# Sixteen chained accumulating scatters in place of a one-hot combination matmul

## The chip, the cores and the metric

One core of one Trainium2 chip runs the whole program. The metric is the device time in microseconds. Beside plain executions there is one profiled execution, from which all rows come.

## What is computed

Two transformer layers on x of 8 images x 256 tokens x 192 channels (2048 tokens in all):

```python
x = x + neighbourhood_attention(ln(x))                 # 12 heads, 7x7 window
t = t + routed(ln(t)) + shared(ln(t))                  # layer 0 mixture of experts
x = x + window_attention(ln(x))                        # rows of 16 tokens
h = x + causal_attention(rms(x)); out = h + moe(rms(h))  # layer 1, 16 experts, top 2
```

The change concerns the routed part of layer 0. Of 32 experts each token chooses 6; an expert keeps at most 48 tokens (CAP), the rest is dropped:

```python
buf_idx = where(pos < CAP, se * CAP + pos, E * CAP)
token_buf = zeros(E * CAP).at[buf_idx].set(tok_of_pair, mode='drop')
xb = x[token_buf].reshape(E, CAP, H)
yb = (silu(g) * u) @ W_down * w_buf[..., None]
routed = zeros((T, H)).at[token_buf].add(yb.reshape(E * CAP, H))
```

## The kernel before, in words

All engines run programs of their own, ordered by semaphores alone; the order of work on each engine is written out by hand. The stages follow each other:

- Stage A, per image: neighbourhood attention, router of layer 0, shared expert. SyncE stores the normalised rows with their router weights (`rows0`), and per image writes zeros over an eighth of `sorted_x` (line 895). TensorE makes slot tables; at the end `ids_f` holds for each of 16 expert pairs (NPAIR) and 128 slots the token's number. A pair has two experts of 64 slots each.
- Stage B, the experts: GpSimd gathers the 16 sets of rows (line 996). The loop `b_body` runs over 8 steps of two pairs: gate and up (lines 1746, 1751), activation, gate product on VectorE (1335), transposes (1765), down (1776). SyncE loads the weights into a ring of five, each load as soon as its slot is read (877, 880). VectorE scales the result by the slot weights into `y_f` (1341), frees the accumulator (`b_yc`), and splits `y_f` into three bf16 parts in `y0_all` (1347 to 1350).
- Stage C, per image: combine, window attention, causal attention, router of layer 1, scatter to `sorted_x` (1031). The combine of an image is `c_comb`: 96 bf16 matmuls of 128 x 128 by 192 (line 1796) with one-hot matrices `comb_s`, which GpSimd compares from `ids_rel` (`c_onehot`, line 1010, 16 per tile and 32 per image); VectorE adds the sum to `x_all` in `c_combine` (1366) and takes the statistics. GpSimd also computes the reciprocal roots of the norms (970, 971), in the same queue as the one-hots.
- In stage C the images overlap by hand: the combine of images 0 and 1 stands ahead of and in the first window attention; in the turn of image i (0 to 5) the combine of image i + 2 stands as 24 matmuls (EARLY_COMB = 8 of 32 steps) ahead of `c_head` and as 72 behind the causal projections (line 1826). The turns of images 6 and 7 have none. VectorE calls `c_combine` of image i + 2 inside the causal attention (`between[1]`).
- Stage F: the 16 experts of layer 1 over 48 sorted tiles; weights of 864 KB a tile, results scattered to `token_y` (1058); then everything is read back, added and stored.

Of the kernel before, what the change touches and what calls it, by code (L numbers as in the profile page):

```python
# [23 lines left out]
P = 128  # L24
# [45 lines left out]
def _lay(table, items):  # L70
    at = 0
    for name, n in items:
# [5 lines left out]
NCF = _lay(CF, [("ident", P), ("iota_slot", CAP), ("iota_tok", P), ("cos", 2 * HD), ("sin", 2 * HD),  # L78
                ("tiles", 16), ("sorted", NSORT), ("half", 2), ("neg", 6), ("back", 1), ("place", NT + 2), ("experts", E1), ("spread", P), ("regions", E1), ("limit", 2), ("dump", 4)])
# [4 lines left out]
def constants():  # L84
# [9 lines left out]
    put(f, CF, "iota_tok", np.arange(P))  # L94
# [9 lines left out]
    put(f, CF, "back", -P)  # L104
# [67 lines left out]
A_FIRST, A_TAIL, C_FIRST = 7, 3, 14  # L172
LINKS = {"A": 32, "B": 5, "C": 62}
C_SHORT = 3
EARLY_COMB = 8


def build(nc, d, out):
    ctx = ExitStack()
    with ctx:  # L180
# [87 lines left out]
        y0_all = y0_words.bitcast(BF16).rearrange("p (j s c) -> p j s c", j=NPAIR, s=3)  # L268
# [14 lines left out]
        comb_s = hT_words.bitcast(BF16).rearrange("p (t j k) -> p t j k", t=2, j=NPAIR)  # L283
# [21 lines left out]
        ids_rel = sb("ids_rel", [P, NPAIR])  # L305
# [57 lines left out]
        token_y = nc.dram_tensor("token_y", [2 * TOK + 2 * P, C], F32)  # L363
        rows0_t = rows0[:, :].rearrange("(i t p) c -> i p t c", t=2, p=P)
# [33 lines left out]
        for n in ("cf_loaded", "cb_loaded", "x0_loaded", "x1_loaded", "x_loaded", "wqkv_loaded", "wproj_loaded", "router_loaded",  # L398
# [4 lines left out]
                  "b_idf", "b_weights", "b_link", "b_done",  # L403
                  "c_onehot", "c_comb", "c_link", "c_var", "c_u", "c_ss", "c_rstd", "c_xn", "c_xT", "c_xTc",
# [5 lines left out]
        for j in range(NPAIR // 2):  # L410
            s(f"b_rows{j}")
        for j in range(RING):
            s(f"ring_gu{j}")
            s(f"ring_dn{j}")
# [445 lines left out]
        def _(sp):  # L860
# [29 lines left out]
            sp.dma_start(sx[NBLOCK - 1], empty).then_inc(s("zeroed"), 16)  # L890
            with sp.Fori(0, B) as i:
# [75 lines left out]
        def _(pool):  # L967
# [31 lines left out]
            pool.wait_ge(s("a_done"), B + 1)  # L999
# [6 lines left out]
            def c_onehot(link, i, t):  # L1006

                nc.gpsimd.tensor_tensor(scratch[:, 9:10], cst("back"), cst("back"), ALU.add)
                for j in range(NPAIR):
                    ins = nc.gpsimd.tensor_scalar(comb_s[:, t, j, :], cst("iota_tok"), ids_rel[:, j:j + 1], None,  # L1010
                                                  ALU.is_equal)
                ins.then_inc(s("c_onehot"), 1)
                pool.wait_ge(s("c_onehot"), 2 * i + t + 1)
                link(nc.gpsimd.tensor_tensor(ids_rel[:, :], ids_rel[:, :], cst("back").to_broadcast([P, NPAIR]),
                                             ALU.add))
            link = Links(pool, s("c_pool"), 0, 8)
# [19 lines left out]
            def c_body(i, level):  # L1036
# [10 lines left out]
                if level == 2:  # L1047
                    c_onehot(link, i + 3, 1)
# [946 lines left out]
```

## Time and profile before

| what | us |
|---|---|
| median of 3 runs (range) | 1319.44 (1316.85 to 1319.55) |
| profiled execution, its own time | 1314.41 |
| its span, first to last instruction | 1312.6 |
| stage A to the first gather | 409.9 |
| stage B, first gather to the last `y_f` | 409.9 to 512.3 |
| stage C to the last scatter of rows | 512.3 to 1094.8 |
| stage F and the end | 1094.8 to 1312.6 |

The mean granted clock of TensorE over the span is 0.94. Read the stages apart: A and F are untouched but for added zero-writes in A; B and C are where every edit lies.

### The profile page before, as it was taken

The numbers are of one execution on the slowest core, as the hardware profiler recorded it, in microseconds if no ns is written. First come the engines' busy times: TensorE is split into PE (matmuls) and PEld (weight loads), VectorE is DVE, ScalarE is ACT, GpSimd is POOL, SyncE is SP. The second block draws the span as 40 slices with busy tenths as digits, with TensorE's granted clock in tenths as the row PEclk, the third lists the DMA queues.
The fourth block names the chain that finished last, engine by engine and source line by source line (L and its number), as shares of the span: only waits on it lengthen the run. The fifth ranks groups of instructions, "written<-read, shape, count | busy, mean of one in ns | idle before, by whom it ended". The sixth has DMA issues, their size and how long they took to land.

```text
span 1312.6 us, 27217 instructions
## 1 busy us (share of the span) xinstructions
PE 1043.5 (80%) x9541; PEld 805.9 (61%) x9573; DVE 747.4 (57%) x2308; ACT 481.1 (37%) x1205; POOL 347.6 (26%) x581
## 2 busy tenths in 40 slices
PE   4899999999987997767777787878767563999992
PEld 3676677677765555646556565656545353888882
DVE  6677668668643443437676767666666644233334
ACT  2454354355342221314454545454535341121120
POOL 0000000000003700683544444444530101233322
PEclk8999999999988999779999999999999775999997
DMA  9044044144229993000000000000000005888885
GB/s 343 13 137 136 3 134 136 33 103 136 59 76 248 372 423 126 0 17 1 15 2 16 0 16 0 16 0 16 0 17 1 17 0 191 270 304 279 281 306 165
DMA packets 69203, 144.73 MB, mean 110 GB/s; under 512 B 4960, under 2 KB 55424, under 8 KB 66848
## 3 DMA queue, kind: packets, MB, share of 16 engines
q1 hardware_dynamic: 64352, 132.76, 30.6%
q0 software_dynamic: 4800, 11.32, 2.6%
q8 instruction: 30, 0.49, 0.2%
q14 instruction: 21, 0.17, 0.0%
HBM read 97.22 MB, written 46.83 MB: 110 GB/s over the span
## 4 chain that ended last, share of the span: by engine, by line
issue 33%; PE 27%; POOL 17%; DVE 12%; ACT 5%; DMA 5%; POOLq 1%; DVEq 0%; ACTq 0%; SPq 0%
POOL R L1010 10%; PE bank L1659 4%; DMA R<-in_ffn_gu 3%; PE bank L577 2%; PE bank L1687 2%; POOL rstd L971 2%; POOL sorted_x L1031 2%; PE bank L595 2%; DVE neg_max L673 2%; PE bank L637 2%; POOL token_y L1058 1%; ACT R L702 1%; PE bank L1796 1%; PE bank L536 1%; PE bank L1746 1%
## 5 line engine op out<-in xcount | busy, mean ns | idle before, releaser
L702 ACT ACTIVATE R<-bank,neg_max 128x128 f32<-128x128 f32 (+2 forms) x576 | 187.6, 410 | 78.1 <-DVE neg_max L673 77.5
L1010 POOL TENSOR_SCALAR R<-cf,ids_rel 128x128 bf16<-128x128 f32 x288 | 187.1, 667 | 0.1
L970 POOL TENSOR_TENSOR rstd<-mean_var,cf 128x2 f32<-128x2 f32 x32 | 6.2, 195 | 612.7 <-DVE mean_var L840 612.4
L673 DVE TENSOR_REDUCE neg_max<-bank 128x2 f32<-128x352 f32 (+2 forms) x216 | 130.1, 611 | 53.5 <-PE bank L560 44.2
L577 PE MATMUL bank<-cf,R 128*128 128x128 f32 x864 | 134.3, 278 | 21.2 <-ACT R L702 12.4
L577 PEld LDWEIGHTS bank<-cf,R 128*128 128x128 f32 x864 | 93.7, 141 | 40.0 <-ACT R L702 13.3
L724 ACT ACTIVATE R<-bank 128x1024 bf16<-128x1024 bf16 x72 | 70.2, 1017 | 106.5 <-PE bank L536 106.5
L1659 PE MATMUL bank<-R 64*116 64x256 f32 (+1 forms) x512 | 97.4, 398 | 0.0
L1574 DVE TENSOR_TENSOR R<-R,bank 128x384 f32<-128x384 f32 x48 | 26.6, 555 | 108.1 <-ACT R L1154 105.4
L1882 PE MATMUL bank<-xsT,R 128*128 128x128 f32 x576 | 75.9, 285 | 13.1 <-DMA R<-in_ffn_w 11.4
L536 PE MATMUL bank<-cb,R 128*128 128x128 bf16 x1008 | 67.5, 230 | 21.8 <-DVE R L521 21.8
L560 PE MATMUL bank<-R 128*128 128x128 bf16 (+2 forms) x576 | 79.4, 243 | 5.3 <-issue 4.6
L1882 PEld LDWEIGHTS bank<-xsT,R 128*128 128x128 f32 x576 | 70.5, 197 | 19.1 <-DMA R<-in_ffn_w 10.9
L1659 PEld LDWEIGHTS bank<-R 64*116 64x116 f32 (+1 forms) x512 | 65.2, 180 | 26.1 <-issue 16.4
L536 PEld LDWEIGHTS bank<-cb,R 128*128 128x128 bf16 x1008 | 62.8, 104 | 28.7 <-DVE R L521 17.9
L1154 ACT ACTIVATE R<-bank 128x384 f32<-128x384 f32 x48 | 23.6, 491 | 142.6 <-PE bank L1889 142.6
L711 ACT ACTIVATE R<-bank 128x512 f32<-128x512 f32 (+2 forms) x152 | 64.4, 461 | 15.1 <-PE bank L577 15.1
L557 PE MATMUL bank<-cb 128*128 128x352 bf16 (+1 forms) x184 | 65.8, 357 | 3.6 <-ACT R L724 3.2
L1796 PE MATMUL bank<-R 128*128 128x192 bf16 x768 | 66.0, 247 | 2.6 <-DVE R L1350 2.6
L560 PEld LDWEIGHTS bank<-R 128*128 128x128 bf16 x576 | 53.0, 103 | 24.6 <-issue 3.6
L1796 PEld LDWEIGHTS bank<-R 128*128 128x128 bf16 x768 | 64.1, 98 | 4.9 <-DVE R L1350 3.0
L595 PE MATMUL bank<-R 128*32 128x128 f32 x1152 | 49.9, 280 | 17.3 <-ACT R L711 17.0
(251 smaller groups left out, 1954.9 us busy)
## 6 DMA issues: line engine op xcount, KB each, us to landing
R<-in_ffn_w SPq DMA_DIRECT2D x48, 864.0 KB, 6.3
sorted_x<-cmp SPq DMA_DIRECT2D x8, 4128.0 KB, 16.9
R<-in_ffn_gu SPq DMA_DIRECT2D x16, 1392.0 KB, 21.3
R<-in_ffn_dn SPq DMA_DIRECT2D x16, 768.0 KB, 18.6
xs_words<-sorted_x SPq DMA_DIRECT2D x48, 129.0 KB, 2.8
R<-token_y SPq DMA_DIRECT2D x8, 384.0 KB, 6.8
rows<-R SPq DMA_DIRECT2D x8, 224.0 KB, 2.2
out_x<-x_all SPq DMA_DIRECT2D x16, 96.0 KB, 2.4
```

The source lines that it names most:

```text
L536: ins = nc.tensor.transpose(bank[:, :].bitcast(BF16)[:, (h * 2 + t) * P:(h * 2 + t + 1) * P], qk_parts[:, row, :, :].rearrange("p s e -> p ...
L557: nc.tensor.matmul(bank[:, 0:len(heads) * kw], cstb("identb"), cstb(mname, moff, len(heads) * kw), start=True, stop=False)
L560: ins = nc.tensor.matmul(bank[:, g * kw:(g + 1) * kw], q_ap(h, t), k_ap(a, h, k0, kw), start=False, stop=(g == len(heads) - 1))
L577: ins = nc.tensor.transpose(PT[u % 2][:, at + g * P:at + (g + 1) * P], probs[:, u % 3, g * kw + c0:g * kw + c0 + P], ident)
L595: ins = nc.tensor.matmul(OB[t][j * HV:(j + 1) * HV, col:col + P], v_ap(a, h, vt), probsT[:, u % 4, at + g * P:at + (g + 1) * P], start=(k ...
L673: nc.vector.tensor_reduce(neg_max[:, u % 4, 0:g], score_bank(u)[:, 0:g * kw].rearrange("p (g k) -> p g k", g=g), AX, ALU.max, negate=True) ...
L702: ins = nc.scalar.activation(probs[:, u % 3, g * kw:(g + 1) * kw], score_bank(u)[:, g * kw:(g + 1) * kw], ACT.Exp, bias=neg_max[:, u % 4, ...
L724: nc.scalar.activation(qkT[:, h0:h0 + heads, :].rearrange("p h t -> p (h t)"), bank[:, :].bitcast(BF16)[:, 0:heads * 256], ACT.Copy, scale ...
L1010: ins = nc.gpsimd.tensor_scalar(comb_s[:, t, j, :], cst("iota_tok"), ids_rel[:, j:j + 1], None, ALU.is_equal)
L1659: ins = nc.tensor.matmul(GATE[g % 3][part][0:DP0, c * 256:(c + 1) * 256], wsgu[rows, 2 if k else part, at:at + DP0], xnT_all[rows, k, :], ...
L1796: ins = nc.tensor.matmul(M1[:, t * C:(t + 1) * C], comb_s[:, t, j, :], y0_all[:, j, k, :], start=(j == 0 and k == 0), stop=(j == NPAIR - 1 ...
L1882: nc.tensor.matmul(GU[r][part][:, c * P:(c + 1) * P], w[:, part * FF + c * P:part * FF + (c + 1) * P], xsT[:, r, 0, :], start=(c == 0), st ...
```

## The change

The 128 weighted rows of a pair, `y_f`, are no longer kept as three bf16 parts. GpSimd adds them to a table `routed` in memory with an accumulating indirect DMA. The table has two halves of 2048 rows, one for the first expert of each pair (slots 0 to 63) and one for the second, and 128 rows behind them for empty slots; so the rows of one scatter are all different. Sixteen scatters run strictly one behind the other (`b_sum`), since two of them can add to the same row. VectorE waits for both scatters of the step before it writes `y_f` again. The table is zeroed by SyncE beside `sorted_x`. Behind the last scatter SyncE loads both halves back per image into `sums` (16 loads of 192 KB), and `c_combine` adds two tiles from there in place of one accumulator. One-hots, the combination matmuls and the bf16 splits are gone. The diff, without the tables of constants, semaphores and tile declarations:

```diff
@@ SyncE
+            sp.dma_start(routed[2 * TOK:2 * TOK + P, :], empty[:, 0:C]).then_inc(s("sum_zeroed"), 16)
             with sp.Fori(0, B) as i:
                 sp.wait_ge(s("a_row"), i + 1)
...
+                sp.dma_start(routed_z[bass.ds(i, 1)].rearrange("a p n c -> (a p) n c"),
+                             empty[:, 0:C].unsqueeze(1).to_broadcast([P, 4, C])).then_inc(s("sum_zeroed"), 16)
...
+            sp.wait_ge(s("b_sum"), 16 * NPAIR)
+            for i in range(B):
+                for k in range(2):
+                    sp.dma_start(sums[:, i, k, :, :], routed_i[i][:, k, :, :]).then_inc(s(f"sum_loaded{min(i, 2)}"), 16)
@@ GpSimd
-            pool.wait_ge(s("a_done"), B + 1)
+            pool.wait_ge(s("sum_zeroed"), 16 * (B + 1))
+            for j in range(NPAIR):
+                pool.wait_ge(s("b_ready"), j // 2 + 1)
+                if j:
+                    pool.wait_ge(s("b_sum"), 16 * j)
+                pool.indirect_dma_start(out=routed[:, :], out_offset=bass.IndirectOffsetOnAxis(ids_s[:, j:j + 1], 0),
+                                        in_=y_f[:, j % 2, :], in_offset=None, compute_op=ALU.add)\
+                    .then_inc(s("b_sum"), 16)
...
-            for i in range(3):
-                if i:
-                    pool.wait_ge(s("c_comb"), 2 * i)
-                    c_root(link, "c_var", i, mv, EPS6)
-                for t in range(2):
-                    c_onehot(link, i, t)
+            for i in range(2):
+                c_root(link, "c_var", i + 1, mv, EPS6)
...
                 if level == 2:
                     c_root(link, "c_var", 2 * i + 4, mv, EPS6)
-                    pool.wait_ge(s("c_comb"), 2 * i + 6)
-                    c_onehot(link, i + 3, 0)
                 c_root(link, "c_ss", 2 * i + 2, ss, EPS6)
-                if level == 2:
-                    c_onehot(link, i + 3, 1)
@@ VectorE
-            nc.vector.tensor_copy(ids_rel[:, :], ids_f[:, :])
             nc.vector.tensor_copy(ids_i[:, :], ids_f[:, :]).then_inc(s("b_idf"), 1)
+            nc.vector.scalar_tensor_tensor(ids_d[:, :], ids_f[:, :], cst("acc"), ids_acc[:, :, 2], ALU.add, ALU.mult)\
+                .then_inc(s("b_link"), 1)
+            dve.wait_ge(s("b_link"), 3)
+            nc.vector.tensor_scalar(ids_s[:, :], ids_d[:, :], cst("limit")[:, 0:1], None, ALU.add)
...
                 dve.wait_ge(s("b_y"), jj + 1)
-                link(nc.vector.tensor_tensor(y_f[:, :, :], two(M1[:, 0:2 * C]),
-                                             wsl[:, bass.ds(2 * jj, 2)].unsqueeze(2).to_broadcast([P, 2, C]), ALU.mult))
...
+                if jj:
+                    dve.wait_ge(s("b_sum"), 32 * jj)
+                nc.vector.tensor_tensor(y_f[:, :, :], two(M1[:, 0:2 * C]),
+                                        wsl[:, 2 * jj:2 * jj + 2].unsqueeze(2).to_broadcast([P, 2, C]), ALU.mult)\
+                    .then_inc(s("b_ready"), 1)
                 nc.vector.memset(scratch[:, 14:15], 0.0).then_inc(s("b_yc"), 1)
-                link(nc.vector.tensor_copy(part(0), y_f[:, :, :]))
-                link(nc.vector.tensor_tensor(y_f[:, :, :], y_f[:, :, :], part(0), ALU.subtract))
-                link(nc.vector.tensor_copy(part(1), y_f[:, :, :]))
-                link(nc.vector.tensor_tensor(part(2), y_f[:, :, :], part(1), ALU.subtract))
...
             def c_combine(link, i):
-                dve.wait_ge(s("c_comb"), 2 * i + 2)
-                link(nc.vector.tensor_tensor(image_x(i), image_x(i), two(M1[:, 0:2 * C]), ALU.add))
+                if isinstance(i, int):
+                    dve.wait_ge(s(f"sum_loaded{i}"), 32)
+                for k in range(2):
+                    link(nc.vector.tensor_tensor(image_x(i), image_x(i), sums[:, bass.ds(i, 1), k, :, :]
+                                                 .rearrange("p a t c -> p (a t) c"), ALU.add))
...
+            dve.wait_ge(s("sum_loaded2"), 32 * (B - 2))
@@ TensorE
-            pe.wait_ge(s("b_done"), LINKS["B"] * (NPAIR // 2))
...
-            c_comb(0, 0, 2 * NPAIR)
             c_head(1)
...
-            attention_pe(pe, WINDOW, 0, {2: lambda: c_comb(1, 0, 2 * NPAIR), (WINDOW.n, "transposed"): lambda: c_head(2)})
+            attention_pe(pe, WINDOW, 0, {(WINDOW.n, "transposed"): lambda: c_head(2)})
...
-                if level == 2:
-                    c_comb(i + 2, 0, EARLY_COMB)
...
-                if level == 2:
-                    c_comb(i + 2, EARLY_COMB, 2 * NPAIR)
```

## Rows read from the trace of the kernel before

**Rows 1.** The longest pieces of the chain that ended last: start us, us, what

```profile
514.30 8.11 PE bank L1796 x96
545.98 7.92 PE bank L1796 x96
570.36 9.27 POOL R L1010 x16
```

**Rows 2.** Windows A:B: length, busy us of each engine (instructions), clock, DMA share, GB/s

```profile
436.10:512.30 76.20, 70.66 (x564) 37.79 (x560) 32.79 (x70) 15.41 (x27) 14.95 (x25) 1.00 0.91 360
909.90:974.70 64.80, 47.62 (x473) 36.40 (x477) 44.01 (x141) 30.60 (x82) 29.65 (x49) 0.97 0.02 8
974.70:1039.30 64.60, 39.77 (x381) 28.86 (x385) 40.09 (x128) 30.07 (x81) 6.84 (x11) 0.89 0.03 9
977.00:986.00 9.00, 3.78 (x11) 2.27 (x10) 6.42 (x25) 0.00 (x0) 2.06 (x3) 0.69 0.14 46
1115.70:1281.00 165.30, 153.47 (x1399) 142.93 (x1398) 52.90 (x218) 33.72 (x88) 49.77 (x85) 1.00 0.84 286
```

**Rows 3.** Timeline, VectorE: start us, us, instruction; first and last y_f, first combine

```profile
436.08 0.56 DVE L1341 TENSOR_TENSOR y_f<-bank,wsl 128x384 f32<-128x384 f32 x1 [2.43 <-PE bank L1776]
...
511.71 0.56 DVE L1341 TENSOR_TENSOR y_f<-bank,wsl 128x384 f32<-128x384 f32 x1 [2.07 <-PE bank L1776]
...
522.53 0.56 DVE L1366 TENSOR_TENSOR x_all<-x_all,bank 128x384 f32<-128x384 f32 x1 [8.29 <-PE bank L1796]
```

**Rows 4.** Timeline of the end, GpSimd's scatter and VectorE's wait for it

```profile
1286.53 0.99 POOL L1058 DMA_INDIRECT token_y<-y_f,place_i  x1 [0.16 <-POOL scratch L1057]
...
1288.91 0.16 DVE L1596 TENSOR_TENSOR place_i<-places,cf 128x1 int32<-128x1 f32 x1 [1.83 <-DMA token_y<-y_f,place_i]
```

**Rows 5.** Line 1058, the 48 scatters of the last stage

```profile
DMA to landing us min/median/max: 2.3/4.8/7.7
```

**Rows 6.** Line 996, the 16 gathers

```profile
DMA to landing us min/median/max: 9.0/12.6/17.2
```

**Rows 7.** DMA issues: count, KB each, median us from issue to landing

```profile
sorted_x<-cmp SPq DMA_DIRECT2D x8, 4128.0 KB, 16.9
...
R<-token_y SPq DMA_DIRECT2D x8, 384.0 KB, 6.8
```

**Rows 8.** Waits from 409 to 530 us: us in total, times, longest

```profile
PE bank L1746 <- DMA R<-in_ffn_gu: 2.4, 2, 1.9
```

**Rows 9.** Timeline, first window attention

```profile
546.43 3.21 ACT L702 ACTIVATE R<-bank,neg_max 128x128 f32<-128x128 f32 x12
...
553.73 0.60 PE L577 MATMUL bank<-cf,R 128*128 128x128 f32 x4
```

**Rows 10.** Timeline, VectorE, after the projection of image 0

```profile
581.20 0.67 DVE L845 TENSOR_SCALAR h_words<-x_all,mean_var,rstd 128x192 f32 x2 [7.77 <-POOL rstd L971]
```

**Rows 11.** Timelines of engines in the turn of image 4

```profile
845.02 1.10 POOL L1031 DMA_INDIRECT sorted_x<-m_row,slots_i  x1 [0.16 <-issue]
...
846.91 2.21 PE L1826 MATMUL bank<-wqkvf,R 96*128 96x288 f32 x8 [0.68 <-ACT R L757]
...
854.71 0.18 DVE L521 COPY R<-R 128x96 bf16<-128x96 bf16 x1
...
854.95 1.85 PE L536 MATMUL bank<-cb,R 128*128 128x128 bf16 x30
...
857.40 0.69 DVE L673 TENSOR_REDUCE neg_max<-bank 128x4 f32<-128x512 f32 x1 [0.91 <-PE bank L560]
```

**Rows 12.** The same in the turn of image 6

```profile
974.76 1.10 POOL L1031 DMA_INDIRECT sorted_x<-m_row,slots_i  x1 [0.16 <-issue]
...
976.64 3.90 PE L1826 MATMUL bank<-wqkvf,R 96*128 96x288 f32 x8 [0.68 <-ACT R L757]
...
985.76 3.38 PE L536 MATMUL bank<-cb,R 128*128 128x128 bf16 x30 [5.22 <-DVE R L521]
...
990.03 2.06 DVE L673 TENSOR_REDUCE neg_max<-bank 128x4 f32<-128x512 f32 x3 [2.00 <-PE bank L560]
```

More of the change, by code:

```diff
@@ L75, in _lay @@
     return at
-NCF = _lay(CF, [("ident", P), ("iota_slot", CAP), ("iota_tok", P), ("cos", 2 * HD), ("sin", 2 * HD),
-                ("tiles", 16), ("sorted", NSORT), ("half", 2), ("neg", 6), ("back", 1), ("place", NT + 2), ("experts", E1), ("spread", P), ("regions", E1), ("limit", 2), ("dump", 4)])
+NCF = _lay(CF, [("ident", P), ("iota_slot", CAP), ("cos", 2 * HD), ("sin", 2 * HD),
+                ("tiles", 16), ("sorted", NSORT), ("half", 2), ("neg", 6), ("acc", 1), ("place", NT + 2), ("experts", E1), ("spread", P), ("regions", E1), ("limit", 2), ("dump", 4)])
 NCB = _lay(CB, [("identb", P), ("tri", P), ("ones", P), ("mask_n", 4 * KW0), ("mask_w", 512),
@@ L103, in constants @@
     put(f, CF, "neg", np.repeat([-0.5, 1e-6, 1e-5], 2))
-    put(f, CF, "back", -P)
+    put(f, CF, "acc", (p >= SLOT)[:, None] * TOK - (2 * TOK + p)[:, None])
     put(f, CF, "place", np.arange(NT + 2)[None, :] * P + p[:, None])
@@ L169 @@
                     (1, 2, 0, 2 * P, [(0, P, 0), (P, P, 1)], ("mask_c1", 0))])
[L172 to L175, printed above, removed]
+A_FIRST, A_TAIL, C_FIRST = 7, 3, 16
+LINKS = {"A": 32, "C": 63}
+C_SHORT = 4
 def build(nc, d, out):
@@ L304, in build @@
         ids_i = sb("ids_i", [P, NPAIR], I32)
-        ids_rel = sb("ids_rel", [P, NPAIR])
+        ids_d = sb("ids_d", [P, NPAIR])
+        ids_s = sb("ids_s", [P, NPAIR], I32)
         scratch = sb("scratch", [P, 32])
@@ L411, in build @@
             s(f"b_rows{j}")
+        for i in range(3):
+            s(f"sum_loaded{i}")
         for j in range(RING):
@@ L1004, in _ @@
             mv, ss = mean_var[:, :, 1], meansq[:, :]
[L1006 to L1016, printed above, removed]
-            for i in range(3):
-                if i:
-                    pool.wait_ge(s("c_comb"), 2 * i)
-                    c_root(link, "c_var", i, mv, EPS6)
-                for t in range(2):
-                    c_onehot(link, i, t)
+            link = Links(pool, s("c_pool"), 0, 2)
+            for i in range(2):
+                c_root(link, "c_var", i + 1, mv, EPS6)
             link.end()
@@ L1027, in c_scatter @@
                 pool.wait_ge(s("c_slots"), i + 1)
-                nc.gpsimd.tensor_tensor(scratch[:, 24:25], cst("back"), cst("back"), ALU.add).then_inc(s("c_go"), 1)
+                nc.gpsimd.tensor_tensor(scratch[:, 24:25], cst("acc"), cst("acc"), ALU.add).then_inc(s("c_go"), 1)
                 for k in range(2):
@@ L1056, in f_body @@
                     pool.wait_ge(s("f_yc"), t + 3)
-                    nc.gpsimd.tensor_tensor(scratch[:, 25:26], cst("back"), cst("back"), ALU.add).then_inc(s("f_go"), 1)
+                    nc.gpsimd.tensor_tensor(scratch[:, 25:26], cst("acc"), cst("acc"), ALU.add).then_inc(s("f_go"), 1)
                     pool.indirect_dma_start(out=token_y[:, :],
@@ L1784, in _ @@
                 b_body(jj, jj + 1 < NPAIR // 2)
-            pe.wait_ge(s("b_done"), LINKS["B"] * (NPAIR // 2))
             pe.wait_ge(s("wc_loaded"), 16 * 3)
             pe.wait_ge(s("wf_loaded"), 16 * 4)
-            def c_comb(i, n0, n1):
-                for n in range(n0, n1):
-                    t, j = divmod(n, NPAIR)
-                    if j == 0:
-                        pe.wait_ge(s("c_onehot"), 2 * i + t + 1)
-                    for k in range(3):
-                        ins = nc.tensor.matmul(M1[:, t * C:(t + 1) * C], comb_s[:, t, j, :], y0_all[:, j, k, :],
-                                               start=(j == 0 and k == 0), stop=(j == NPAIR - 1 and k == 2))
-                    if j == NPAIR - 1:
-                        ins.then_inc(s("c_comb"), 1)
             def c_head(k, bank=S0):
```

19 lines of the change are left out of this document (8 added, 11 removed).

## The prediction, before the change was run

> **What bounds the kernel now.** I read the chain that ended last first, because busy shares mix stages. What the reader is to see there: the combine that this change removes stands in the chain at two early places, as 8.1 us of matmuls of line 1796 behind the last expert pair and 7.9 us inside the first window attention, and a one-hot stretch of GpSimd of 9.3 us follows [rows 1]. Then the windows, stage by stage, because the stages have different limits. In the expert stage the DMA engines are 91% busy and TensorE 93%; in a loop turn with combines TensorE is busy 47.6 us of 64.8 at a mean clock of 0.97; the turn of image 6, which has no combine and no one-hot, takes 64.6 us at 0.89 [rows 2]. That last pair is the most telling: a turn without this work was not shorter. Last, the timeline at each place where the new chain has to fit.
>
> **Expert stage: what goes, what comes.** Four VectorE steps per pair (the bf16 split) go. They run in a shadow: the eight y_f lie 75.6 us apart from first to last [rows 3], 10.8 us a step, and TensorE (93% busy) and the weight loads set that, so I cost their removal at nothing. What comes is a lock-step chain: y_f written (0.56 us), scatter, scatter, and only then may VectorE write y_f again. Behind that waiting instruction on VectorE stand the gate products of the next pair, for these TensorE's transposes and down matmuls wait, and for those SyncE's weight loads; so if the chain is longer than 10.8 us it sets the pace.
>
> The price of one scatter: on quiet DMA engines a 128 x 768 B scatter lands 2.4 us after its issue began (1286.53 to 1288.91) [rows 4]. Beside the weights of the last stage (DMA 84% busy [rows 2]) the same scatter has a median of 4.8 and a maximum of 7.7 us [rows 5]. The gathers beside the zero-writes and weights ahead of the expert stage needed 9.0 to 17.2 us, but they also queue behind each other [rows 6]. Nothing shows what the addition costs (the destination has to be read too): between nothing and one more trip of 2.4 us; I take 0.5. Issue and landing are both inside these figures; I add 0.1 us for each wake-up. Lower bound: 0.6 + 2 x 2.5 = 5.6 us a step, hidden under 10.8. At the median: 0.6 + 2 x 4.9 = 10.4 us, just hidden. At the maximum: 0.6 + 2 x 7.8 = 16.2 us, so +5.4 us a step, +38 us over seven. At 9.0: 18.8 us, +56 us. The load of the expert stage is above that of the last stage (91% over the stage, and full until its weights are in), but a longer pace thins it, so the ends pull together; I take 5.5 for the trip and 0.5 for the addition, 0.6 + 2 x 6.1 = 12.8 us a step, seven of them 89.6 us in place of 75.6: **+14 us**. The Trainium skill (DMA: Bandwidth & Descriptors, section Anatomy of one DMA) gives a software-issued DMA a fixed 2.0 us plus bytes over 436 GB/s whatever else runs, which is an estimate of 2.2 us for these 96 KB. The quiet row agrees, the loaded rows do not; by that rule the chain would be hidden, which is the first rival below.
>
> If the chain is hidden, the stage still gets more bytes. The added zero-write per image is 384 KB; at the rate of the zero-writes that are there (4128 KB in 16.9 us [rows 7]) 1.6 us, of which that of the last image stands ahead of the weights of the stage. Fourteen scatters before the last weights carry 1.4 MB out and as much is read for the addition, 4 to 8 us at the 360 GB/s of that stage [rows 2]. TensorE already waits for weights (2.4 us in two waits [rows 8]), so this shows: about +6 us. It is contained in the +14, since a stage paced by the chain leaves the DMA engines idle time.
>
> **From the last pair to the first image.** Before: last y_f at 511.7, combined image at 522.5, 10.8 us [rows 3]. After: 0.6 for y_f, two scatters on quiet engines 2 x 3.0, then SyncE's first two loads of 192 KB. Loads of 384 KB, eight in a row, land in 6.8 us [rows 7]; for half the bytes and nothing ahead of them I take 3.3, plus a second VectorE addition of 0.55 and 0.3 of wake-ups: 10.8 us. **0 us**, bounds -2 and +5. The other fourteen loads are not waited for until the middle of the first window attention, some 30 us later.
>
> **First window attention.** The 96 matmuls of image 1 go (7.9 us [rows 1]). TensorE resumed at 553.7; it would then wait for ScalarE's first four exponentials, a third of twelve that take 3.21 us from 546.43, so until 547.5 [rows 9]. **-6 us**, bounds -5 and -7.5.
>
> **The root behind the one-hots.** VectorE waited 7.77 us for the reciprocal root of image 0, which stood behind 9.3 us of one-hots in GpSimd's queue [rows 1, 10]. GpSimd is free now: **-7.7 us**, bounds -7 and -9. In the loop the roots find GpSimd idle, so nothing more comes from there.
>
> **The loop, six turns with combines.** In a turn, 24 matmuls fill the wait for the normalised rows and 72 the wait for the query and key splits: VectorE's last split starts at 854.71 and takes 0.18, TensorE is at it at 854.95 [rows 11]. So the direct gain is 0.1 us. What they did do is keep TensorE going. In the turn of image 6 nothing stands there, and the same matmuls of line 1826 take 3.90 us in place of 2.21, TensorE waits 5.22 us, the 30 transposes take 3.38 in place of 1.85 [rows 11, 12], at a granted clock of 0.69 over those 9 us [rows 2]: more than half of the time at the lower level (1.2 GHz), the rest at 2.4. From the turn's first scatter to the first maximum 12.38 us became 15.27, a loss of 2.9 us. That this turn came out at 64.6 and not 67.5 is because the combine, statistics and normalisation of the image after next are missing from it (VectorE is busy 3.9 us less [rows 2]); in the changed kernel's turns they are there. So a turn loses up to 2.9; the dip in the first gap needs the gap to fall as it did, the one in the second is near certain (1.8 of the 2.9). I take 2.3. The second addition costs 0.55 in VectorE's fullest stretch, and the splits there get faster without one-hots beside them: of the 3.9 us that VectorE is busy less in the turn of image 6 some 2.4 are instructions that are absent, and of the other 1.5 I put 0.7 on the path. One dip of the old turn, late in it, may go: -0.2. So 2.3 + 0.55 - 0.7 - 0.1 - 0.2, about 2.0, six times: **+12 us**, bounds 0 (the clock holds) and +20.
>
> **Sum.** +14 + 0 - 6 - 7.7 + 12 = +12.3 us. The profiled execution took 1314.4 us (span 1312.6 and 1.8 around it), 5.0 below the median of the three runs, 1319.44; carried to that median: 1332 us, slower by 0.9%.
>
> **Rivals.**
> 1. The chain is hidden, the clock is still lost. For it: the median of [rows 5] gives 10.4 us, and a pace of 10.8 holds it. Against: no addition is in that, and the stage is busier. +6 in place of +14: +4.3, 1324 us.
> 2. Faster: the chain is hidden and the clock holds, because the old turn's dips and the new ones trade places. Against: image 6. For: a single turn is thin evidence, and only where low activity falls decides it. +6 + 0 - 6 - 7.7 + 0 = -7.7, 1312 us. It decides for faster once stage and loop together cost under 11 us, that is at a step of at most 11.7 us and a loop turn that loses under 0.8.
> 3. The chain is fully exposed: 7.7 us and more per trip, since a scatter meets two bursts of weights per step. +38 (to +56) in place of +14: 1356 to 1374 us. Against: at 16 us a step the weights need 10 of them, so the engines are half free.
>
> That the change does not do what it says is no case: the matmuls and one-hots are simply gone.
>
> **Chances and range.** The forecast 0.45, rival 1 0.2, rival 2 0.2, rival 3 0.15. About 0.2% (2.6 us) is what a measurement of this kernel can tell from no change. Faster: rival 2 and a little from the edge of rival 1, 0.24; within 0.2%: the strip between them, 0.06; slower 0.70. The range reaches from rival 2 to the near end of rival 3, 1312 to 1360; the forecast's own is 1325 to 1344.
>
> **What the profile after would show.** The y_f writes 12 to 14 us apart with VectorE waiting for the scatter (right), or at 10.8 to 11.7 (rival 1), or at 16 and more (rival 3); a trip of 5 to 7 us in the stage and of 2.4 to 3.5 for the last two. The first combined image 10 to 13 us behind the last y_f. The root of image 0 with no wait of 7.8 us. Loop turns of 66 to 68 us in place of 64.8 with line 1826's matmuls at 3.9 us and a clock near 0.9; turns of 64.8 or less would show the clock step wrong. What would upset all of it: an issue that itself takes much longer than 1 us with an addition in it, or an addition that takes the DMA engines several times a plain write.

## The result and the profile after

| | before | after |
|---|---|---|
| median on the same chip, us (4 runs each) | 1319.05 | 1357.69 |
| range of the runs after, us | | 1351.58 to 1359.10 |
| profiled execution: its own time, span, us | 1314.41, 1312.6 | 1357.57, 1355.5 |
| mean granted clock of TensorE | 0.94 | 0.893 |

The ratio is 1.0287, with a 95% interval from 1.0254 to 1.0321: slower by 38.6 us. The forecast was 1332, so 12.6 above the median that it started from. The sign came out as predicted and the time lies in the stated range of 1312 to 1360, but it lies outside the forecast's own 1325 to 1344, and the loss is three times the forecast. An execution can also fall into a slower state with a lower clock, as one of run 6's five did; its ratio leaves that one out. Part by part, between the two profiled executions, whose own times lie 43.2 us apart (the first y_f after stands 2.6 us later than before, a difference ahead of the stage and within what executions differ by: 436.1 to 441.7 in the twelve traces):

| stretch | before | after | difference | forecast |
|---|---|---|---|---|
| start to first y_f | 436.1 | 438.7 | +2.6 | 0 |
| first to last y_f | 75.6 | 107.1 | +31.5 | +14 |
| last y_f to first combined image | 10.8 | 11.9 | +1.1 | 0 |
| first combined image to first scatter of rows | 61.65 | 50.8 | -10.8 | -13.7 |
| six turns of the loop | 390.6 | 409.8 | +19.3 | +12 |
| the rest | | | -0.7 | 0 |

**The expert stage.** The chain that ended last, through this stage of the changed kernel; the columns are start us, length us, what. A DMA piece runs from the start of its issue to its landing.

```profile
438.72 0.57 DVE y_f L1344
440.11 12.26 DMA routed<-y_f,ids_s
452.41 0.74 issue
453.15 9.35 DMA routed<-y_f,ids_s
462.59 0.57 DVE y_f L1344
463.43 9.18 DMA routed<-y_f,ids_s
472.64 0.71 issue
473.35 9.39 DMA routed<-y_f,ids_s
482.83 0.57 DVE y_f L1344
...
536.68 0.57 DVE y_f L1344
537.25 0.27 issue
537.51 3.52 DMA routed<-y_f,ids_s
541.07 1.10 issue
542.18 3.54 DMA routed<-y_f,ids_s
545.81 0.57 DVE y_f L1344
```

From the first y_f to the last the chain does not pass through TensorE. It alternates between a write of y_f and two scatters, and 0.71 us or more pass from a landing to the next issue. A trip takes 7.4 to 12.3 us beside streaming weights and 3.4 to 3.6 us where few bytes move (from 528.0 to 545.8 the DMA engines are 22% busy and move 24 GB/s). The step from 462.59 to 482.83 is 20.2 us long, the one from 536.68 to 545.81 is 9.1. The waits from 409 to 560 us (engine, line and what it waited for: us in total, times, longest) name the same place, and the windows show what the engines made of it (length, busy us of each engine with its instructions, clock, DMA share, GB/s):

```profile
DVE y_f L1344 <- DMA routed<-y_f,ids_s: 69.5, 7, 16.4
```

```profile
438.70:545.80 107.10, 78.62 (x564) 41.59 (x560) 17.93 (x41) 15.51 (x27) 21.79 (x14) 0.86 0.76 269
...
545.80:557.70 11.90, 0.00 (x0) 0.00 (x0) 0.57 (x2) 0.00 (x0) 3.10 (x2) 0.66 0.34 63
...
881.90:950.20 68.30, 47.25 (x405) 33.89 (x405) 44.02 (x142) 30.76 (x82) 7.68 (x14) 0.88 0.02 8
884.00:888.00 4.00, 3.68 (x8) 2.10 (x7) 1.82 (x8) 0.00 (x0) 2.13 (x3) 0.57 0.27 99
891.00:898.00 7.00, 5.11 (x42) 4.44 (x43) 3.08 (x11) 3.08 (x4) 0.00 (x0) 0.52 0.00 0
904.60:908.20 3.60, 3.57 (x26) 1.86 (x27) 2.98 (x6) 2.03 (x5) 0.00 (x0) 0.53 0.00 0
925.00:928.70 3.70, 3.59 (x20) 2.96 (x21) 2.03 (x4) 2.38 (x6) 0.00 (x0) 0.54 0.00 0
```

Every y_f but the first waits for the scatters, 69.5 us in all. TensorE has the same 564 matmuls in the stage as before and is busy 8 us longer, at a clock of 0.86 in place of 1.00; the DMA engines fell from 91% [rows 2] to 76% busy. So neither of the engines that had set the pace does so now.

**The loop.** The last five windows are one turn of image 4, and four stretches in it in which the clock is near its lower level (1.2 GHz). The first two lie at the waits that the combination matmuls had filled. The timeline of that turn, to be read beside [rows 11, 12]:

```profile
883.78 3.90 PE L1810 MATMUL bank<-wqkvf,R 96*128 96x288 f32 x8 [0.68 <-ACT R L760]
892.89 3.38 PE L539 MATMUL bank<-cb,R 128*128 128x128 bf16 x30 [5.21 <-DVE R L524]
...
892.65 0.18 DVE L524 COPY R<-R 128x96 bf16<-128x96 bf16 x1
...
897.16 1.50 DVE L676 TENSOR_REDUCE neg_max<-bank 128x4 f32<-128x512 f32 x2 [2.00 <-PE bank L563]
```

The projections of line 1810 (1826 before) take 3.90 us, the wait for the splits is 5.21, the transposes take 3.38: to 0.01 us what the turn of image 6 had shown before [rows 12]. From the turn's first scatter (881.89) to its first maximum pass 15.27 us, also as there. The third stretch, in the causal attention, has no counterpart in the argument: at the same place of the turn before the clock is 1.00. It is there in the turns of images 3, 4 and 5 (68.15 to 68.26 us) and absent in that of image 2 (67.36 us). The fourth is the late dip that the old turn has too (0.58 from 885.0 to 888.7).

### The profile page after: what moved, and what is told of

Read it like the earlier page. It is cut to its first block, busy times and chain, and to the rows that moved or that the text cites. A ratio compares the mean times of both kernels' runs of the same rounds, so it can differ in the third digit from the quotient of the medians.

```text
span 1355.5 us, 25402 instructions
## 1 busy us (share of the span) xinstructions
PE 1025.9 (76%) x8805; PEld 769.0 (57%) x8805; DVE 731.5 (54%) x2285; ACT 481.7 (36%) x1205; POOL 177.0 (13%) x273
## 4 chain that ended last, share of the span: by engine, by line
issue 43%; PE 23%; DVE 12%; DMA 9%; POOL 7%; ACT 5%; POOLq 0%; DVEq 0%; SPq 0%; ACTq 0%
DMA routed<-y_f,ids_s 7%; PE bank L1659 4%; PE bank L580 2%; PE bank L1687 2%; POOL sorted_x L1034 2%; PE bank L598 2%; DVE neg_max L676 2%; POOL rstd L981 2%; PE bank L640 2%; PE bank L539 1%; ACT R L705 1%; POOL token_y L1057 1%; PE bank L769 1%; PE bank L776 1%; PE bank L560 1%
## 5 line engine op out<-in xcount | busy, mean ns | idle before, releaser
L705 ACT ACTIVATE R<-bank,neg_max 128x128 f32<-128x128 f32 (+2 forms) x576 | 187.0, 406 | 80.7 <-DVE neg_max L676 80.3
L580 PE MATMUL bank<-cf,R 128*128 128x128 f32 x864 | 136.5, 281 | 20.5 <-ACT R L705 13.9
L539 PE MATMUL bank<-cb,R 128*128 128x128 bf16 x1008 | 78.2, 249 | 52.8 <-DVE R L524 52.8
L539 PEld LDWEIGHTS bank<-cb,R 128*128 128x128 bf16 x1008 | 72.7, 114 | 64.0 <-DVE R L524 53.7
L560 PE MATMUL bank<-cb 128*128 128x512 bf16 (+1 forms) x216 | 84.7, 392 | 0.6 <-ACT R L727 0.2
L563 PE MATMUL bank<-R 128*128 128x128 bf16 (+2 forms) x576 | 83.2, 252 | 0.0
L1864 PEld LDWEIGHTS bank<-xsT,R 128*128 128x128 f32 x576 | 69.1, 194 | 19.8 <-issue 10.8
L563 PEld LDWEIGHTS bank<-R 128*128 128x128 bf16 x576 | 55.9, 108 | 27.9 <-issue 9.4
L598 PE MATMUL bank<-R 128*32 128x128 f32 x1152 | 50.2, 281 | 15.5 <-ACT R L714 15.3
L755 PE MATMUL bank<-cf,R 128*96 128x128 f32 x100 | 17.1, 297 | 54.0 <-DVE R L848 28.7
L769 PE MATMUL bank<-wqkv,R 96*128 96x384 f32 x128 | 54.2, 576 | 1.4 <-ACT R L760 1.4
L1687 PE MATMUL bank<-R 116*128 116x192 f32 x256 | 53.3, 330 | 0.3 <-DVE R L1285 0.3
```

Source lines behind the costliest of these rows:

```text
L539: ins = nc.tensor.transpose(bank[:, :].bitcast(BF16)[:, (h * 2 + t) * P:(h * 2 + t + 1) * P], qk_parts[:, row, :, :].rearrange("p s e -> p ...
L560: nc.tensor.matmul(bank[:, 0:len(heads) * kw], cstb("identb"), cstb(mname, moff, len(heads) * kw), start=True, stop=False)
L563: ins = nc.tensor.matmul(bank[:, g * kw:(g + 1) * kw], q_ap(h, t), k_ap(a, h, k0, kw), start=False, stop=(g == len(heads) - 1))
L580: ins = nc.tensor.transpose(PT[u % 2][:, at + g * P:at + (g + 1) * P], probs[:, u % 3, g * kw + c0:g * kw + c0 + P], ident)
L598: ins = nc.tensor.matmul(OB[t][j * HV:(j + 1) * HV, col:col + P], v_ap(a, h, vt), probsT[:, u % 4, at + g * P:at + (g + 1) * P], start=(k ...
L705: ins = nc.scalar.activation(probs[:, u % 3, g * kw:(g + 1) * kw], score_bank(u)[:, g * kw:(g + 1) * kw], ACT.Exp, bias=neg_max[:, u % 4, ...
```

## The experiments

Each run was timed beside executions of the kernel before on the same chip, whose medians were between 1318.97 and 1322.95 us. Runs 1, 2, 3 and 5 are single executions. Those of one kernel spread over up to 1%, so these four are read by their traces, and the total stands beside it.

**1. Without the addition.** The scatters overwrite.

```diff
-                                        in_=y_f[:, j % 2, :], in_offset=None, compute_op=ALU.add)\
+                                        in_=y_f[:, j % 2, :], in_offset=None)\
```

> The changed kernel with the addition left out of the sixteen scatters: they are chained as before but overwrite their rows, so the routed sum holds one expert's row per half instead of up to six. In the changed kernel the eight y_f lie 107.1 us apart and a scatter takes 3.5 us on quiet DMA engines (a plain one of the same shape 2.4). Theory A, the trips are long because they share the DMA engines with the weights: each trip gets only 1.1 us shorter, 14 of them, so y_f first to last is 88 to 95 us and loaded trips of 6 to 11 us remain; total about 1342. Theory B, the addition is what is slow under load (it must read the destination): loaded trips fall to the 4.8 us of the last stage, y_f first to last 76 to 80 us, total about 1328.

Measured: 1339.09 us in one run. The y_f lie 94.2 us apart from first to last (107.1 with the addition) and the median trip over the whole chain is 6.0 us. From the chain of this kernel:

```profile
458.18 6.11 DMA routed<-y_f,ids_s
465.06 6.04 DMA routed<-y_f,ids_s
...
533.96 2.34 DMA routed<-y_f,ids_s
537.07 2.35 DMA routed<-y_f,ids_s
```

Both figures of a plain scatter are there: 2.34 us quiet, as [rows 4] had it, and mostly some 6 beside the weights (5.8 to 10.0), against a median of 4.8 in [rows 5]. The addition costs 1.2 us on quiet engines (3.54 against 2.34) and about 3 beside the weights. The issue instruction also differs, and it lies inside these trips. The group of line 1014 in the changed kernel, and then in this one (ns, min/median/max):

```profile
L1014 POOL DMA_INDIRECT routed<-y_f,ids_s x16: 1548/1548/1635, 440.1 to 550.9; - x16
```

```profile
L1014 POOL DMA_INDIRECT routed<-y_f,ids_s x16: 972/972/1002, 440.3 to 537.1; - x16
```

The issue takes 0.58 us longer with the addition, so about half of the quiet 1.2 us is GpSimd's and not the DMA engines'. In the stage the addition accounts for 13 us of the 31.5, and the lock-step of plain scatters beside weights for the other 18.6 (94.2 against 75.6). The 75.6 is itself loose by some 2 us: with the same expert stage, runs 5 and 10 took 73.5 and 73.2.

**2. Without the weights.** The chain is complete, with its additions; the weights of pairs 5 to 15 are not loaded, and these pairs use what lies in the ring. The waits of TensorE go to the first load of each slot.

```diff
-                    load_gate_up(j)
...
-                    load_down(j)
...
-                pe.wait_ge(s(f"ring_gu{j % RING}"), 16 * (j // RING) + 16)
+                pe.wait_ge(s(f"ring_gu{j % RING}"), 16)
...
-                pe.wait_ge(s(f"ring_dn{j % RING}"), 16 * (j // RING) + 16)
+                pe.wait_ge(s(f"ring_dn{j % RING}"), 16)
```

> The changed kernel without the weight loads of expert pairs 5 to 15 in the first mixture (these pairs use the weights left in the ring), so the DMA engines carry nearly only the scatters in the expert stage. Theory A (queueing behind weights): every trip falls to 3.5 us, a step to 0.6 + 2 x (3.5 + 0.8) = 9.2 us, below TensorE's pace, so y_f first to last is 72 to 76 us and the total about 1325. Theory B (the addition itself): trips of 7 us and more remain in places, y_f first to last stays over 95 us.

Measured: 1320.89 us in one run; the stage takes 73.1 us, the median trip is 3.5. The whole stage of this kernel in one window, and its last scatters in the chain:

```profile
437.40:510.50 73.10, 70.53 (x564) 37.75 (x560) 18.40 (x41) 15.41 (x27) 21.79 (x14) 1.00 0.31 59
```

```profile
511.35 3.50 DMA routed<-y_f,ids_s
514.88 0.71 issue
```

TensorE is busy 96% of the stage at full clock, and is the bound again. The same sixteen scatters add nothing to the stage once the weights of eleven pairs are gone from the queues: what is expensive in it is the meeting of chain and weights. The loop turns stayed at 67.7 to 68.3 us in both runs, so the loss there has a cause of its own.

**3. VectorE released.** All sixteen y_f lie side by side in the memory of the old bf16 parts, and VectorE waits for no scatter.

```diff
-                                        in_=y_f[:, j % 2, :], in_offset=None, compute_op=ALU.add)\
+                                        in_=y_all[:, j, :], in_offset=None, compute_op=ALU.add)\
...
-                if jj:
-                    dve.wait_ge(s("b_sum"), 32 * jj)
-                nc.vector.tensor_tensor(y_f[:, :, :], two(M1[:, 0:2 * C]),
+                nc.vector.tensor_tensor(y_all[:, 2 * jj:2 * jj + 2, :], two(M1[:, 0:2 * C]),
```

> The changed kernel with sixteen y buffers in place of two: VectorE no longer waits for scatters, the chain is the same. Theory A: the experts' pace comes back (y_f first to last 75 to 80 us), but the chain then runs beside full weight loads, 9 to 11 us a trip while they last, and catches up at 4.3 us a scatter: last landing 535 to 555 us, total 1340 to 1357. Theory C, the loss is the lock step between VectorE and the scatters (two buffers only): the last landing follows the last y_f by two trips, near 525 us, total about 1328.

Measured: 1353.0 us in one run, which is inside the changed kernel's own 1351.58 to 1359.10. The y_f now lie 79.9 us apart, but the scatters did not keep up. From the chain of this kernel:

```profile
502.35 9.57 DMA routed<-R,ids_s
512.67 3.55 DMA routed<-R,ids_s
...
547.34 3.57 DMA routed<-R,ids_s
```

The first seven took 8.9 to 11.8 us each, one behind the other, while the weights streamed, and the last landed at 550.9, against 554.5 in the changed kernel. The wait had moved from VectorE to the end of the chain. The order of the scatters among themselves is the constraint, and VectorE's wait was only where it showed.

**4. Idle matmuls in the gaps of the loop.** They multiply constants into columns of the accumulator that nobody reads, 24 ahead of `c_head` and 72 behind the causal projections, as many as the combine had there.

```diff
+            def keep_busy(n):
+                for m in range(n):
+                    nc.tensor.matmul(M1[:, (m % 2) * C:(m % 2 + 1) * C], cstb("identb"), cb[:, 0:C], start=True, stop=True)
...
+                if level == 2:
+                    keep_busy(24)
                 c_head(2 * i + (3 - short(i)), M0)
...
                     ins.then_inc(psem("qkv", CAUSAL), 1)
+                if level == 2:
+                    keep_busy(72)
                 transpose_qk(pe, CAUSAL, i)
```

> The changed kernel with 24 and 72 idle matmuls (128 x 128 by 192, bf16, of constants, into columns of the accumulator that nobody reads) at the two places of each loop turn where the combination matmuls stood. Theory D, the turn grew from 64.8 to 68.3 us because TensorE's clock falls in the two gaps: turns come back to 64.8 to 65.6 us, the six turns to under 394 us (409.8 in the changed kernel, 390.6 before), total 1338 to 1342, 1.2 to 1.4 % under the changed kernel. Theory E, the turn grew because VectorE has a second addition per image and reads from SBUF: turns stay at 68 us or get longer by up to the 0.2 us by which the matmuls outlast the splits; total 1357 or more.

Measured: 1334.52 us (1331.59 to 1335.35), a ratio to before of 1.0104 [1.0070, 1.0138], 23 us under the changed kernel. The six turns take 388.3 us in place of 409.8. One turn in the windows, and TensorE in it:

```profile
866.34:931.07 64.73, 49.49 (x497) 38.30 (x501) 43.92 (x142) 30.55 (x82) 7.63 (x14) 0.97 0.02 8
```

```profile
868.23 2.21 PE L1816 MATMUL bank<-wqkvf,R 96*128 96x288 f32 x8 [0.68 <-ACT R L760]
870.27 6.11 PE L1790 MATMUL bank<-cb 128*128 128x192 bf16 x72
876.21 1.84 PE L539 MATMUL bank<-cb,R 128*128 128x128 bf16 x30
```

Work that computes nothing made the changed kernel faster, and by more than its expectation had it (1338 to 1342): the projections are back at 2.21 us and the transposes at 1.84. With the clock restored the six turns are 2.3 us shorter in sum than before, all of it in the first; the other five sum to 324.1 us in both. So the rest of the change, the second addition and the absent one-hots together, costs no time in the loop on balance. Of the 23 us the turns are 21.5.

**5. The clock alone, on the kernel before.** In the turns each combine is cut to its last matmul per tile, so that images 2 to 7 get only a fraction of their routed part. One-hots, splits and everything else stay.

```diff
+                    if short_comb and j < NPAIR - 1:
+                        continue
-                    for k in range(3):
+                    for k in range(1 if short_comb else 3):
...
```

> The kernel before, unchanged but that in the six loop turns the combine of an image is one matmul per tile in place of 48 (so 2 in place of 96; the routed sum of images 2 to 7 is that of one pair only). Scatters, added loads and a second VectorE addition are all absent. Theory D (the clock): turns grow from 64.8 to 67.8 to 68.5 us, the total to about 1337 to 1340 us, with fewer instructions than before. Theory E (the second addition, reads from SBUF): turns stay at 64.8 or fall to 64.6, total 1317 to 1319.

Measured: 1334.54 us in one run. A stretch of a turn's length in the windows:

```profile
651.90:719.30 67.40, 45.34 (x405) 33.18 (x408) 44.06 (x141) 30.81 (x82) 29.50 (x49) 0.87 0.02 8
```

The six turns sum to 411.1 us (70.66, 67.42, 68.77, 67.74, 68.78, 67.76) against 390.6: +20.5 from the removal of matmuls alone, at a clock of 0.87 in that stretch, and without any chain, table or load. Run 5 adds 20.5 us to the kernel before, run 4 takes 21.5 from the changed one: the loop's +19.3 is the clock.

**6. Two tables.** Even pairs add to one, odd pairs to the other, so only scatters of the same table wait for each other. It needs twice the zero-writes, 32 loads and four additions per image.

```diff
-                if j:
-                    pool.wait_ge(s("b_sum"), 16 * j)
-                pool.indirect_dma_start(out=routed[:, :], out_offset=bass.IndirectOffsetOnAxis(ids_s[:, j:j + 1], 0),
+                if j >= 2:
+                    pool.wait_ge(s(f"b_sum{j % 2}"), 16 * (j // 2))
+                pool.indirect_dma_start(out=routed[j % 2][:, :], out_offset=bass.IndirectOffsetOnAxis(ids_s[:, j:j + 1], 0),
...
```

> The changed kernel with two tables: even pairs are added to the one, odd pairs to the other, so the two scatters of a step run at the same time and each waits only for the one two before it. Costs: twice the zero-writes and loads, four additions per image on VectorE in place of two. If the chain's trips are the cost, a step takes one loaded trip of 9 to 12 us plus 1.4, y_f first to last 80 to 90 us, and the gap from the last y_f to the first combined image falls from 11.9 to about 9 us: total 1330 to 1340. If what counts is what the scatters take from the DMA engines (bytes and turns), two at once are no faster than two in a row: total 1355 or more.

Measured: 1346.56 us over all five executions, 1344.25 over the four without the profiled one (1338.86 to 1346.92), ratio 1.0188 [1.0158, 1.0217]. That is 13.4 us under the changed kernel, and above the 1330 to 1340 expected. The profiled one took 1366.43 us at a clock of 0.875, so its turns are not read; the y_f lie 88.8 us apart in it, 18 less than in the changed kernel and as expected. Each scatter is about as slow beside another as alone (median trip 8.9 us in run 7, which has the same tables, against 8.9 to 9.6 for those alone behind the first in run 3), so two in flight hide one behind the other.

**7 to 9. The parts combined.** Run 7 has two tables, sixteen buffers and the 24 and 72 idle matmuls; run 8 is the same with one table; run 9 is run 7 with 48 and 108. The edits are those of runs 3, 4 and 6, and for run 9

```diff
-                    keep_busy(24)
+                    keep_busy(48)
...
-                    keep_busy(72)
+                    keep_busy(108)
```

> Two tables, sixteen y buffers and the idle matmuls in the loop turns, together: y_f first to last 78 to 82 us, each strand of eight scatters keeps up with the experts, last landing 5 to 7 us behind the last y_f, first combined image 5 to 8 us later than in the kernel before, then 10.8 us regained up to the first turn, turns of 64.8 to 65.5 us (two more additions than in e4): total 1314 to 1322, no clear difference to the kernel before. If the strands do not keep up with the weights' load: 1325 to 1335.

> The changed kernel with one table, all sixteen addition buffers apart (VectorE does not wait for scatters) and the same 24 and 72 idle matmuls in the loop turns that the run of the changed kernel with idle matmuls had. The run with two tables had the same idle matmuls and turns of 68.1 to 70.3 us, with 1.15 us more of additions in each turn. Theory A (the idle matmuls hold the clock only where the turn's own gaps are as short as they are with two additions; the 1.15 us of the second table's additions bring the half clock back): turns of 64.2 to 65.1 here, and a time of 1353.0 - 1357.6 + 1334.5, some 1330 us. Theory B (the second buffers, thus the early end of the expert stage, change how the clock falls in the loop): turns of 67 us and more here, and 1346 to 1351 us.

> The kernel with two tables, sixteen buffers and idle matmuls, with 48 and 108 idle matmuls in a turn in place of 24 and 72. If more filling brings back the clock there, turns fall from 68.4 to 65 or 66 us (64.8 and the 1.15 us of added additions) and the time from 1350 to 1328 to 1335 us. If the half clock falls in stretches where none of this filling lies (behind the sorted feed-forward's start and at the gates of the mixture, as the trace of the earlier run has it), turns stay at 68 to 70 us, or get longer by the matmuls, and the time stays at 1348 us or more.

| run | median us | ratio to before | first to last y_f | turns of the loop |
|---|---|---|---|---|
| 7: two tables, 24 and 72 | 1349.98 | 1.0229 [1.0201, 1.0256] | 84.0 | 68.1 to 70.3 |
| 8: one table, 24 and 72 | 1335.5 | 1.0104 [1.0071, 1.0137] | 80.7 | 64.7 to 65.0 |
| 9: two tables, 48 and 108 | 1360.83 | 1.0297 [1.0253, 1.0342] | 81.7 | 69.3 to 75.2 |

Run 7 came out 28 us above its expectation of 1314 to 1322: the turns should have been under 66 us. Four windows of 6 us from a turn of it:

```profile
732.00:738.00 6.00, 5.81 (x82) 5.70 (x81) 4.11 (x14) 1.52 (x2) 0.00 (x0) 1.00 0.00 0
738.00:744.00 6.00, 3.16 (x25) 1.81 (x23) 5.06 (x14) 3.47 (x11) 0.52 (x2) 1.00 0.00 0
744.00:750.00 6.00, 5.13 (x44) 3.15 (x46) 5.63 (x10) 3.88 (x11) 0.39 (x1) 0.72 0.00 0
...
768.00:774.00 6.00, 6.00 (x42) 4.90 (x40) 3.85 (x9) 4.99 (x18) 0.00 (x0) 0.53 0.00 0
```

Where the idle matmuls stand the clock is full; it falls later, in the attention, where no gap had been foreseen. With one table and everything else equal the turns are back at 64.8 us, as the first theory of run 8 had it. What differs in a turn are the additions on VectorE: four, which take 2.65 us from start to end, in place of two in 1.25. Behind them VectorE copies the tile that TensorE waits for. The additions and that wait, first in run 7 (turn of image 3), then in run 8 (turn of image 2):

```profile
808.15 2.65 DVE L1368 TENSOR_TENSOR x_all<-x_all,R  x4
812.97 0.66 PE L599 MATMUL bank<-R,v_causal 128*32 128x128 f32 x8 [2.44 <-DVE R L650]
```

```profile
742.40 1.25 DVE L1363 TENSOR_TENSOR x_all<-x_all,R  x2
745.82 0.43 PE L599 MATMUL bank<-R,v_causal 128*32 128x128 f32 x8 [1.04 <-DVE R L650]
```

TensorE waits 1.40 us longer, which is what the two more additions take, and the matmuls behind the wait take 0.66 us in place of 0.43: the clock is down. The wait is 2.44 or 2.45 us in each of run 7's first five turns, with the 0.66 or 0.65 right behind it in four of them, and 1.04 in run 8's first five, with 0.43. So the traces show where the clock is lost and by which wait; the additions were not varied alone. Run 8's ratio is that of run 4, so the sixteen buffers brought nothing that these times can tell. With more idle matmuls (run 9) the clock came back to 0.98 and 0.95 in two turns, but the turns did not, and this is plain in the timeline:

```profile
813.97 9.07 PE L1794 MATMUL bank<-cb 128*128 128x192 bf16 x108
822.88 1.84 PE L540 MATMUL bank<-cb,R 128*128 128x128 bf16 x30
```

VectorE's last split had ended at 819.85 and the transposes start at 822.88: 3 us of filling on the path. That turn has the clock of 0.98 and takes 69.3 us, 4.5 more than run 8's; the longer additions are 1.4 of it.

**10. The kernel before, with one stretch of one-hots moved.** This takes the useful part of the change alone: the roots of the first turn are put ahead of 16 of the one-hots that they waited for [rows 1, 10].

```diff
-                for t in range(2):
+                for t in range(2 if i < 2 else 1):
                     c_onehot(link, i, t)
...
                 c_root(link, "c_ss", 2 * i + 1, ss, EPS6)
+                if first:
+                    c_onehot(link, 2, 1)
                 c_scatter(i)
```

> The kernel before with one thing moved: the sixteen one-hots of image 2, tile 1 stand behind the two roots of image 0's first turn in GpSimd's queue, not ahead of them. It takes from the change the only part that paid without the chain. If VectorE's 7.77 us of waiting for the root were all on the path: 1311 to 1313 us, 0.5 % faster. If TensorE's combine of image 2 then waits for the moved one-hots (they end about 6 us later against its need): a gain of 0 to 4 us, 1315 to 1319.

Measured: 1315.6 us (12 runs) against 1319.08 (17 runs), ratio 0.9973 [0.9951, 0.9995]. The interval just leaves out no change. VectorE no longer waits for the root, but the moved one-hots now stand ahead of the first scatter of rows, and TensorE's combine waits for them:

```profile
592.84 1.10 POOL L1031 DMA_INDIRECT sorted_x<-m_row,slots_i  x1 [0.33 <-issue]
```

```profile
592.00 4.13 PE L1802 MATMUL bank<-R 128*128 128x192 bf16 x48 [3.13 <-POOL R L1010]
```

The wait has moved more than it has gone. From the first combined image to the second turn's first scatter it is 127.67 us, against 128.12 before, and by the end of the six turns no gain is left in this execution (1320.59 us, among the longest of the twelve). The median is the only one under both kernels', by 0.3%; the trace does not show where that comes from, and it is not more than a hint.

## What the prediction had right, and which step failed

**Which mechanisms.** All those of the forecast are there: the chain sets the pace of the stage, the clock falls in the loop's gaps, the attention and the root give back time. Rival 1 (chain hidden) and rival 2 (hidden and clock held) are out: VectorE waited 69.5 us for scatters. Rival 3 (7.7 us and more per trip, chance 0.15) describes four of the seven steps, which took 23.9, 20.2, 18.5 and 17.9 us; the other three took 8.7 to 9.1. The total is rival 3's as well (1356 to 1374), but not for its reason alone: its loop cost 12 us and the measured one 19.3. No step lies at the 12 to 14 us that were to show the forecast right.

**The step that failed: the price of the expert stage, +14 forecast, +31.5 measured.** The sum was 0.6 + 2 x (5.5 + 0.5 + 0.1) = 12.8 us a step; the measured mean is 107.1 / 7 = 15.3. Adding up the fourteen trips of the chain before the last y_f gives 94.0 us, 6.7 each in place of 6.0, so 10 us more; the 13.1 us that remain are 1.87 a step in place of 0.8, another 7.5. Three terms in particular:
- The trip beside weights, put at 5.5. Without the addition it is mostly 6.1 us (run 1), so this alone was near; with it, 7.4 to 12.3. The trace's median of the sixteen accumulating trips is 5.5, but that is chance: none lies between 3.7 and 7.3.
- The addition, put at 0.5. It is 1.2 us quiet (run 1 against the changed kernel), in the bounds of nothing to 2.4, and about 3 us beside weights, outside them. The bound was a round trip on quiet engines. Of either figure 0.58 us is the longer issue, which the prediction named as a sign and had no term for. That the rest grows under load shows in run 1; the reason was not taken apart.
- The wake-up, put at 0.1 each. From a landing to the next issue on GpSimd it is 0.71 (once 1.10), seven times in the stage, and 0.27 from the end of a y_f to an issue.

What the single figure lacked is the split between 7 to 12 us beside weights and 3.5 without. The remark that a longer pace thins the traffic was right: the steps of 9 us kept the mean under rival 3's 16.2 a step.

**From the last pair to the first image: 0 forecast, +1.1.** Two scatters of 3.5 us and the gap of 0.71 cost 1.8 more than the 6.0 taken for them; the loads landed in 2.67 us, faster than the 3.3. Inside the bounds.

**First attention and root: -13.7 forecast, -10.8.** The wait for the root is gone. From the first to the second combined image it was -4.7 (forecast -6), from there to the scatter -6.2 (forecast -7.7). For 1.2 of the 2.9 us missing a row of before and one of after show the place. The projections of the next image run at the lower clock for part of their time, and VectorE, whose next instruction is the normalisation that had waited for the root, waits for them:

```profile
569.47 3.36 PE L766 MATMUL bank<-wqkv,R 96*128 96x384 f32 x8
```

```profile
600.50 4.59 PE L769 MATMUL bank<-wqkv,R 96*128 96x384 f32 x8
605.12 0.56 DVE L789 TENSOR_TENSOR R<-bank,brow 128x384 f32<-128x384 f32 x1 [1.26 <-PE bank L769]
```

Another 1.0 us are three groups of matmuls on both chains behind the first combined image (lines 755, 776 and 539 after): 1.08, 1.90 and 4.78 us in place of 0.89, 1.44 and 4.41. TensorE had no matmul from the last y_f to that image (window 545.80 to 557.70), where the combine had stood before. So most of the miss is the clock again, which the prediction had charged to the loop alone; 0.7 us were not traced to rows.

**The loop: +12 forecast, +19.3, inside its bound of +20.** The reasoning from the turn of image 6 held to the hundredth of a microsecond: 15.27 us to the first maximum. The prediction's terms add up to 1.85 us a turn, 11.1 in six, which it rounded to 2.0 and 12. Measured it is 3.2 a turn. The clock's term was under-sized at 2.3: its removal is worth 3.6 us a turn in run 4 and 3.4 in run 5. Of the turn of image 4, 2.9 are lost by the first maximum, as the row that the prediction had read says, and 0.4 behind it, where the third stretch lies; the first turn lost 4.95 alone. The other terms (0.55 for the second addition, 0.7 back for the splits, 0.1 and 0.2) were to give 0.45 back, and run 4 shows nothing given or taken by their sum in five turns; it does not split them.

The Trainium skill (TensorE: Matmul & The Clock Gate, section HAM oscillation — how this bites in real kernels) says that a loop whose waits between groups of matmuls are long enough falls to the lower clock in every pass. Runs 4 and 5 agree, at some 3.5 us a turn.

**The rule that was weighed.** The Trainium skill (DMA: Bandwidth & Descriptors, section Anatomy of one DMA) gave an estimate of 2.2 us for these bytes. Plain scatters on quiet engines agree (2.34), accumulating ones do not (3.5), and beside weights neither kind does (6, and 7 to 12).

**Open.** Whether the second table's additions alone bring the low clock back, since they were not varied alone, why the third stretch is missing in one turn, and what an accumulating scatter does inside the DMA engines.

## What to carry to other kernels

A chain of dependent DMAs is priced by what its engines carry at that moment: take its trip from rows beside the same traffic, add the issue of the next (0.7 us from a landing here), and put it where the engines are quiet, or expect two to three times the quiet price. Matmuls that stand in a wait are not free to remove: look at the granted clock around a turn without them first, and if it falls, fill the wait, but not beyond it. And before moving a piece of work to clear a queue, look at who waits for the piece: in run 10 TensorE did, 3.1 us, and next to nothing was won.

## What the runs showed of the hardware

- An accumulating indirect scatter of 128 rows of 768 B costs GpSimd 1.55 us to issue, a plain one 0.97. From the start of its issue it lands in 3.5 us against 2.3 on quiet engines, and in 7.4 to 12.3 us against 5.8 to 10.0, mostly 6.1, beside streaming weights (changed kernel and run 1).
- Two such scatters in flight beside weights take about as long each (median 8.9 us, run 7) as one alone (8.9 to 9.6 behind the first, run 3).
- 96 idle matmuls a turn raised the granted clock from 0.88 to 0.97 and shortened a turn from 68.3 to 64.7 us; 156 of them, in the kernel with two tables, gave 0.98 and 0.95 in two turns, which were 69.3 and 70.9 us long.
- In the causal attention a wait of TensorE of 2.44 us in place of 1.04 was followed by matmuls at the lower clock (0.66 us in place of 0.43; runs 7 and 8, in four turns of the five looked at).
